# Attention and FP8 feed-forward block: batch 0 ahead of the other batches, maxima half a batch ahead of the exponentials, and shift rows copied in quarters

## The reference

```python
    x = L0_attn_X
    xn = _layernorm(x, axis=-1)
    x = x + _L0_attn_ref(xn, W_q, W_k, W_v, W_o) + _L0_ffn_ref(xn, weight, bias)

    # attention: Qr, Kr are the rotated projections, per head of width 16
        scores = jnp.einsum('bhqd,bhkd->bhqk', Qr, Kr) * DH ** (-0.5)
        scores = jnp.where(causal[None, None], neg, scores)
        pattern = jax.nn.softmax(scores, axis=-1)
        heads = jnp.einsum('bhqk,bhkd->bhqd', pattern, Vh)
        out = heads.transpose(0, 2, 1, 3).reshape(b, t, d)
        return out @ W_o.T
    # linear layer
        def fake_quant_fp8(t):
            amax = jnp.max(jnp.abs(t))
            scale = FP8_E4M3_MAX / jnp.maximum(amax, 1e-12)
            q = (t * scale).astype(jnp.float8_e4m3fn).astype(jnp.float32)
            return q / scale
        xq = fake_quant_fp8(x); wq = fake_quant_fp8(weight)
        return jnp.einsum('bsd,od->bso', xq, wq) + bias
```

## Time and profile before

| | us |
|---|---|
| median of 3 runs | 468.52 (466.98 to 469.78) |
| the profiled execution's own time | 468.62 |
| its span | 466.9 |
| PE busy | 405.5 (87%) |
| DVE busy | 350.1 (75%) |
| ACT busy | 277.3 (59%) |
| POOL busy | 274.4 (59%) |

### The profile page before, as it was taken

One profiled execution on the slowest core, in us unless ns is written; L12 is line 12 of the kernel. 1 busy time (PEld: TensorE's weight loads), 2 busy tenths in 40 slices (PEclk: granted clock), 3 DMA queues, 4 the chain that ended last, 5 costly groups with the idle time before them and its releaser, 6 DMA issues.

```text
span 466.9 us, 9145 instructions
## 1 busy us (share of the span) xinstructions
PE 405.5 (87%) x2819; PEld 222.8 (48%) x2819; DVE 350.1 (75%) x1340; ACT 277.3 (59%) x500; POOL 274.4 (59%) x278
## 2 busy tenths in 40 slices
PE   1790676999889999999999999999999999998975
PEld 1440521364345556654565556555655545643443
DVE  3779899969769977997799778977897878842041
ACT  2742932147765677567666765677567656675850
POOL 2304376636746984698459844985498337226552
PEclk9996555599999999999999999999999999999999
DMA  7826747300483238422851375037504760020021
GB/s 234 257 87 197 159 136 193 81 5 18 143 214 84 69 101 204 131 69 78 216 144 46 93 213 152 32 110 206 158 18 124 194 170 2 4 93 3 1 91 46
DMA packets 37617, 53.43 MB, mean 114 GB/s; under 512 B 5152, under 2 KB 31136, under 8 KB 37536
## 3 DMA queue, kind: packets, MB, share of 16 engines
q1 hardware_dynamic: 37568, 52.84, 40.6%
HBM read 35.78 MB, written 17.04 MB: 113 GB/s over the span
## 4 chain that ended last, share of the span: by engine, by line
PE 44%; POOL 22%; ACT 11%; issue 10%; DVE 8%; DMA 3%; POOLq 1%; SPq 1%; ACTq 0%; DVEq 0%
PE st_ps L842 10%; PE o_ps L922 9%; PE s_ps L860 7%; ACT prob L722 6%; PE m_ps L894 5%; PE m_ps L869 4%; POOL prob L427 4%; POOL rot L259 4%; PE m_ps L798 4%; POOL rot L253 3%; DVE scratch L587 3%; POOL xq L457 3%; POOL parts L263 3%; POOL rot L252 2%; POOL qv L453 2%
## 5 line engine op out<-in xcount | busy, mean ns | idle before, releaser
L587 DVE CUSTOM_DVE_ANT_0 scratch<-s_ps,causal 128x512 bf16<-128x512 f32 (+3 forms) x512 | 220.9, 485 | 55.0 <-PE s_ps L860 52.9
L722 ACT ACTIVATE prob<-st_ps 128x512 f32<-128x512 f32 x320 | 174.8, 600 | 97.9 <-PE st_ps L842 97.4
L427 POOL TENSOR_SCALAR_AFFINE_SELECT prob<-prob 128x512 f32<-128x512 f32 (+1 forms) x160 | 86.4, 544 | 130.9 <-ACT prob L722 129.4
L860 PE MATMUL s_ps<-k_st,q_st 96*128 96x512 bf16 (+3 forms) x512 | 130.8, 320 | 7.0 <-DVE rowmax L587 3.2
L842 PE MATMUL st_ps<-q_st,k_st 98*128 98x128 bf16 (+3 forms) x512 | 121.9, 303 | 4.2 <-ACT prob L722 2.8
L922 PE MATMUL o_ps<-prob,v_sb 128*17 128x512 f32 (+3 forms) x1024 | 87.4, 437 | 10.0 <-ACT heads L737 5.1
L842 PEld LDWEIGHTS st_ps<-q_st,k_st 98*128 98x128 bf16 x512 | 42.0, 97 | 76.3 <-ACT prob L722 42.3
L860 PEld LDWEIGHTS s_ps<-k_st,q_st 96*128 96x128 bf16 x512 | 48.9, 99 | 43.7 <-DVE rowmax L587 20.6
L922 PEld LDWEIGHTS o_ps<-prob,v_sb 128*17 128x17 f32 x1024 | 20.5, 96 | 48.3 <-issue 36.0
L587 DVE DVE_READ_ACCUMULATOR2_ANT rowmax<- 128x1 f32 x512 | 41.7, 81 | 0.1
L894 PE MATMUL m_ps<-wo_sb,attnT 128*128 128x256 f32 x128 | 33.2, 381 | 1.8 <-DVE x_res L610 1.4
(11 more groups left out here) (99 smaller groups left out, 502.6 us busy)
## 6 DMA issues: line engine op xcount, KB each, us to landing
qk_parts<-parts SPq DMA_DIRECT2D x16, 768.0 KB, 3.7
q_st<-qk_parts SPq DMA_DIRECT2D x32, 192.0 KB, 3.3
k_st<-qk_parts SPq DMA_DIRECT2D x32, 192.0 KB, 3.7
q_st<-x_dram SPq DMA_DIRECT2D x8, 512.0 KB, 5.5
q_st<-qk_parts SPq DMA_DIRECT2D x32, 128.0 KB, 3.4
k_st<-qk_parts SPq DMA_DIRECT2D x32, 128.0 KB, 3.7
x_res<-x_dram SPq DMA_DIRECT2D x8, 512.0 KB, 3.5
out_dram<-x_res SPq DMA_DIRECT2D x8, 512.0 KB, 4.8
```

The source lines that it names most:

```text
L427: eng.affine_select(out=ap, in_=ap, compare_op=ALU.is_ge, fill=0.0, base=0, pattern=pat, channel_multiplier=-1).then_inc(masked, 1)
L587: eng.tensor_tensor_reduce(scratch[:, at, col:col + w], s_ps[at][:, col:col + w], causal[:, T - w:T], 1.0, NEG, ALU.add, ALU.max, rowmax[: ...
L722: eng.activation(prob[u][:, half * T:(half + 1) * T], st_ps[ST_BANK[2 * s + half]][:, :], ACT.Exp, scale=SCALE).then_inc(exp_done, 1)
L860: mm = eng.matmul(bank[:, col:col + (qb + 1) * P], q_st[0:ROWS, 1 - par, h, qb * P:(qb + 1) * P], k_st[0:ROWS, 1 - par, h, 0:(qb + 1) * P] ...
```

## The change

Time is counted in slots of the exponentials: slot 20n+s is slot s of batch n. The lists now run from slot -10 to 175.

- **Start.** Only batch 0 is normalised, turned, projected and split first, with its parts handled in halves, on DVE and POOL; batch 1 is normalised beside it. The statistics, normalising and turning of batches 3 to 7 stand in the slots -9 to 8 (`LATE_NORM` is the slot of the turning), that of batch 2 just ahead. The largest value per batch (`largest`) follows in the odd slots 1 to 15, the scales in slots 16 to 20.
- **Maxima** run 10 slots ahead of the exponentials (`LEAD`), where it was 20. Slots -10 to -1 hold maxima alone.
- **The table** `OFFSETS` takes the place of `MISC`: the slot of each item relative to its batch's first. `o`, `at` and `fin` come 2 to 5 slots sooner, `qk` stands in every second slot from 10 to 16, `mt` is in four quarters of 16 columns (two halves of 32 before).
- **Rounding** of batch n moves from slots 20 to 26 of its count to 16 to 20 (`quant_slot`); batch 0's is at 23 to 27.
- **Rotation and split** on POOL move from slots 3 to 13 of an iteration to slots 13 to 22 (`rotate` at 13 and 18, `remainder` 15 and 20, `low` 17 and 22).
- **Shift rows** go from SBUF to SBUF, two DMAs a quarter (write and read through DRAM before, in halves).
- **Stacks** are written as before and read in halves of 8 heads, at slots 0, 3, 5 and 8 of the batch before (groups of 4 heads before): 12 reads a batch where there were 24.
- **End.** The last batch's output is stored in four parts.

```diff
+OFFSETS = {("v", 0): 0, ("mt", 1): 1, ("v", 1): 2, ("o", 0): 23, ("o", 1): 24, ("o", 2): 25, ("mt", 2): 6, ("o", 3): 26,
+           ("at", 0): 26, ("at", 1): 27, ("fin", 0): 28, ("at", 2): 29, ("fin", 1): 30, ("qk", 0): -30, ("mt", 3): 11,
+           ("at", 3): 31, ("fin", 2): 32, ("qk", 1): -28, ("qk", 2): -26, ("fin", 3): 34, ("qk", 3): -24, ("mt", 0): -4}
+LATE_NORM = {2: -8, 3: -6, 4: -4, 5: -2, 6: 3, 7: 7}
...
+def quant_slot(n):
+
+    return 23 if n == 0 else SLOTS * n + 16
...
+            def write_parts(n, w):
+
+                eng.wait_ge(low_done[w], 2 * n + 2)
+                eng.dma_start(qk_dram[n % 2, w].rearrange("t r j h n -> (j h) (t r) n"),
+                              parts[:, w].rearrange("p t r n -> p (t r) n")).then_inc(parts_out[w], 16)
...
+            def shift_rows(n, g):
+
+                c = NG * n + g
+                eng.wait_ge(shift_done, c + 1)
+                for t in range(SHIFT):
+                    eng.dma_start(q_st[ROWS + t:ROWS + t + 1, n % 2, g * HG:(g + 1) * HG, :],
+                                  shift[:, t, :]).then_inc(shift_in[c % 2], 16)
...
+                for off, step, w in ((-27, rotate, 0), (-25, remainder, 0), (-23, low, 0),
+                                     (-22, rotate, 1), (-20, remainder, 1), (-18, low, 1)):
+                    n = batch_at(slot, off, 1)
+                    if n is not None:
+                        step(eng, n, w)
...
+                for n in quant_at(slot, 2):
+                    eng.wait_ge(qc_done, n + 1)
+                    eng.tensor_tensor(qv[:, :], qv[:, :], qe[:, :], ALU.add).then_inc(qw_done, 1)
+                for n in quant_at(slot, 4):
+                    eng.wait_ge(qw_done, n + 1)
+                    wait_past(eng, full["fin"], 4 * n)
+                    eng.tensor_tensor(xq.rearrange("p c t -> p (c t)"), qv[:, :], qe[:, :],
+                                      ALU.subtract).then_inc(xq_done, 1)
```

More of the change, by code:

```diff
@@ L61, in wait_past @@
         eng.wait_ge(sem, count)
-def each_batch(eng, step, between):
-    for n in range(NB):
-        step(n, n % 2)
-        between(n)
 def unit_parts(u, half):
@@ L198, in attention_ffn_block @@
         s_full = sem("s_full")
-        full = {k: sem(f"{k}_full") for k in ("qk", "v", "o", "at", "fin", "mt")}
+        full = {k: sem(f"{k}_full") for k in ("qk", "v", "o", "at", "fin", "mt", "spread", "ln")}
         pv_done = sem("pv_done")
@@ new lines, in _ @@
+            statistics(0)
+            statistics(1)
+            eng.wait_ge(w_qk_in, 16 * 4)
+            rope(0, 0, first_ps[0])
+            rope(0, 1, first_ps[1])
+            rotate(eng, 0, 0)
+            rope(0, 2, first_ps[2])
+            rope(0, 3, first_ps[3])
+            rotate(eng, 0, 1)
+            remainder(eng, 0, 1)
+            low(eng, 0, 1)
+            statistics(2)
+            for slot in range(FIRST_SLOT, END_SLOT):
+                at = maximum_slot(slot)
+                if at is not None:
+                    n, s = at
+                    row_max(n, 2 * s)
+                    row_max(n, 2 * s + 1)
+                for n in range(3, NB):
+                    if slot == LATE_NORM[n] - 3:
+                        statistics(n)
+                if slot in range(1, 2 * NB, 2):
+                    largest(slot // 2)
+                weight_step(slot)
+                for kind, n, k in shared_at(slot, "qk", "o", "fin", "mt"):
+                    {"qk": rope, "o": norm, "fin": finish, "mt": split_max}[kind](n, k, shared[kind, n, k])
+                for n in quant_at(slot, 1):
+                    eng.wait_ge(qv_done, n + 1)
+                    eng.tensor_scalar(qe[:, :].bitcast(U32), qv[:, :].bitcast(U32), 0x7F800000, None,
+                                      ALU.bitwise_and).then_inc(qe_done, 1)
+                    eng.wait_ge(qe_done, n + 1)
+                    eng.tensor_scalar(qe[:, :], qe[:, :], 2.0 ** -6, 1.5 * 2.0 ** 20, ALU.max, ALU.mult)\
+                       .then_inc(qc_done, 1)
@@ new lines, in high_x, with exp @@
+            def high_x(n):
+                wait_past(eng, full["qk"], 4 * n if n > 1 else 0)
+                eng.copy(x_parts[:, 0], xnT[:, n]).then_inc(x_high, 1)
+            def exp(n, s):
+                g, u = divmod(s, 5)
+                if n > 0 or g > 0:
+                    eng.wait_ge(pv_done, 12 * n + 3 * (g - 1) + (1, 1, 2, 2, 3)[u])
+                for half in range(2):
+                    eng.wait_ge(st_full, 2 * (SLOTS * n + s) + half + 1)
+                    eng.activation(prob[u][:, half * T:(half + 1) * T], st_ps[ST_BANK[2 * s + half]][:, :],
+                                   ACT.Exp, scale=SCALE).then_inc(exp_done, 1)
@@ new lines, in copy_at @@
+            def copy_at(n, qb, bank):
+                eng.wait_ge(full["at"], 4 * n + qb + 1)
+                wait_past(eng, full["fin"], 4 * n + max(qb - 1, 0))
+                eng.copy(attnT[:, qb % 2, :, :], bank[:, 0:D].rearrange("p (c n) -> p c n", c=NC))\
+                   .then_inc(at_copied, 1)
+            nw = NC * D
+            normalise(0)
+            copy_turned(0)
+            normalise(1)
+            high(0, 0)
+            copy_turned(1)
+            middle(0, 0)
+            high(0, 1)
@@ L974, in _, with scores @@
-            run(iteration)
+            def scores(n, s, between):
+                g, u = divmod(s, 5)
+                if u == 0:
+                    c = NG * n + g
+                    eng.wait_ge(shift_in[c % 2], 32 * (c // 2 + 1))
+                for half in range(2):
+                    i = 2 * s + half
+                    wait_past(eng, exp_done, HALVES * n + ST_BEFORE[i] + 1)
+                    for j, kb, col in unit_parts(u, half):
+                        h = g * HG + j
+                        mm = eng.matmul(st_ps[ST_BANK[i]][:, col:col + T - kb * P],
+                                        k_st[0:ROWS + SHIFT, n % 2, h, kb * P:(kb + 1) * P],
+                                        q_st[0:ROWS + SHIFT, n % 2, h, kb * P:T], start=True, stop=True)
+                    mm.then_inc(st_full, 1)
+                    if half == 0:
+                        between()
```

996 lines of the change are left out of this document (451 added, 545 removed).

## The result

| | before | after |
|---|---|---|
| median of 4 runs each | 468.04 us (466.98 to 469.78) | 525.78 us (524.48 to 526.42) |
| ratio, 95% interval | | 1.123 (1.118 to 1.127) |
| span of the profiled execution | 466.9 us | 524.2 us |
| mean granted clock | 0.938 | 0.909 |

The kernel is 12.3% slower. The prediction had the sign, slower, but its time was 480, its range ended at 490, and 57.7 us were lost where it said 12.

What follows compares the result with a forecast made beforehand. PE bounds the middle, DVE the start's maxima. 121.5 to slot 20, 236.3 middle, 17.5 and 3.7 added there, 42.7 and 40.0 for batches 6 and 7, 16.5 tail: 478.2, plus 1.7 is 480 us; range 463 to 490.

Steps and rivals of the forecast that it cites:

- The start: Up to slot 20: first maximum at 40.5, slot 0 at 67.0, slot 20 at 121.5 instead of 134.3, a gain of 12.8.
- Slots -10 to -1: Maxima ahead of slot 0: DVE 25.0 us, PE 29.8 at half clock; 26.5 taken, between 25 and 30.
- Batch 0: Slots 0 to 19: DVE's work sums to 53.1 us, 1.4 for waits makes 54.5, where it took 44.5.
- Rival (c): PE's clock stays at half in batch 0: slot 20 at 144, time 503 us; chance 0.03.
- (e): The start isn't won, first maxima wait for the reads until 50: 489 us; chance 0.12 together with Rival (d).
- Direct copies and larger stack reads: Shift rows from SBUF to SBUF and stack reads of 8 heads: 0 each; far end for the copies 1 a batch.
- Rival (d): The direct copies of the shift rows come late: 7 us more, 487 us; chance 0.12 together with (e).
- Part 1: Middle, slots 17 to 23: POOL's 13.9 us chain makes PE wait 3.0 a batch, with 0.6 more through ACT and DVE.
- the mask in slot 23: Sign in the middle: PE waits over 2 us a batch for the mask, at the products with V.
- `qe`: Rounding on DVE in slot 17, beside `low`: contention counted as 0.65, as beside POOL's rotation (1.34 against 0.69 alone).
- Part 2: Slot 6: `at` waits for `split_max`, a bank passed on in the same slot, 1.3 a batch.
- the first `fin`: Once, in slot 28: held by POOL's second addition and the bias sum, 2.7.

Runs made afterwards that it cites:

- e1: The changed kernel with the second halves of Q's and K's stacks read 12 and 6 slots ahead, not 17 and 12: 502.32 us, ratio 1.071.
- e4: The changed kernel with twelve extra PE products before the wait for the third quarter of the shift rows, batches 2 to 6: 516.40 us, ratio 1.099.
- e10: e6 with ScalarE's scaling for the rounding back in slot 16 instead of 17: 478.51 us, ratio 1.020.
- e11: e10 with batches 2 and 3 normalised and turned, batch 3's statistics and three `largest` computed ahead of the first maximum: 472.47 us, ratio 1.006.
- e5: e1 with the rounding of batches 1 to 7 spread over slots 17 to 25, the two `qe` apart: 485.60 us, ratio 1.037.
- e6: e5 with the first transpose of the attention output in slot 27 instead of 26: 479.05 us, ratio 1.021.
- e3: The changed kernel with all steps of the rounding one slot sooner: 523.22 us, ratio 1.114.

## Why the prediction was wrong

**The start: order right, 6.8 us too early.** The first maximum was late by 2.5 us: the first half of K was issued at 34.5 and landed at 43.0, on full engines (share 1.05), with both second halves issued behind it by 38.5. I had 7.3 us for the reading back; it took 8.5 and began 1.3 us later than I had it. Slots -10 to -1 took 30.6, just above the end of my bracket of 25 to 30: PE waited 7.8 us there for rotation products that stand on DVE behind statistics, in a bank that it needed in the same slot. I had summed each engine by itself and taken a value near the larger sum; in a stretch where two engines pass banks back and forth, each has gaps that the other's queue makes. Batch 0 was right to 0.2 us, partly by luck: DVE was busy for 50.1 us, not 53.1, and idle for 4.6, not 1.4. Its busy share was 92%, where the prediction had named over 95% as the sign. Rival (c), half a clock through batch 0, didn't come (0.95), and (e) came in part.

**Direct copies and larger stack reads, both costed at nothing: the step that failed.** "Larger stack reads: 0, they are 3 us or more early" asked whether the stacks are in time, and they were. It didn't ask what else is in the DMA engines while they run. In batch 4 of the new order three half reads of 768 KB each are issued from 313.6 to 322.7, and the split of the third quarter (slot 6) and its use (slot 10) lie in the time that these take. Rival (d) had the right place of trouble but a price from the wrong row: it took 3.7 us, a large transfer alone in the earlier trace rows, as the longest a copy could take, and up to 9.1 us are what a copy took beside the reads. e1 puts the price of this step at 23.5 us. No run reads the stacks in groups of 4 heads again, so what their size did, apart from their place, isn't shown.

**The clock, left out of the middle.** I used the clock for the start and for rival (c), and charged waits in the middle at their length. PE's waits of 2.7 to 3.9 us were followed by stretches at half. In the middle the clock is 0.92 over 288.7 us, so that some 46 us passed at half and some 23 us of work were lost, beside the 33 us of waits themselves. e4 shows this by itself: more work in the wait, less time.

**Part 1, POOL's chain: found, smaller, and hidden behind something else.** It costs 1.44 a batch (e10, e11), through ScalarE, where I had 3.0 at the mask and 0.6 for ScalarE and DVE. In the changed kernel it doesn't show, I suppose because PE waits longer, 2.70, for DVE in the same slots. The prediction named the mask in slot 23 as its sign, and POOL made no PE wait there.

**`qe`: the rule was right and the row that I took was not the case at hand.** I weighed 0.65 us of contention from the earlier trace rows against the whole `low`, and let the sum stay. `qe` began 0.11 us behind `low` and took 2.58: its own 0.68 and the remaining 2.02 of `low` give 2.70. Beside the shorter rotations it took 1.4 to 1.8, alone 0.67. The Trainium skill, "SBUF — State Buffer", section "SBUF: two separate sides", says that of DVE and POOL the one that starts first on their shared port pair keeps it for its whole instruction, and the other waits. The trace agrees: 2.58 us, with 2.70 by that rule. The row of 1.34 was a `qe` that started at 240.81 beside a rotation of 1.27 us begun at 240.33; what was left of that, 0.79, is about the 0.65 that I took for a constant. With the clock and the row of maxima behind it, this step and the place of the rounding cost 16.7 us (e5), where I had 0.6 a batch, some 3 us in all, for it and ScalarE together.

**Part 2, a bank passed on in the same slot: right.** 1.3 a batch was said, 1.14 measured, with DVE's split as releaser, and e6 gets 6.6 us back for it. It is the one new wait that the order alone made plain. Of what comes once, PE's wait in front of the first `fin` was 0.5 and not 2.7.

In numbers, from the changed kernel on: 23.5 us for the stack reads beside the shift rows, 16.7 for the rounding, 6.6 for the bank, 6.0 for work that the start could have done while it waited, and 0.5 from e6 to e10, which is within noise. That leads from 525.8 to 472.5. 3 us over before remain. The middle of e11 loses 2.4 us a batch against before, 12 in all, which takes back the 12 us by which its slot 20 is earlier (V projection at 123.4 against 135.3), and from 371.6 to the end it takes 99.2 us where before took 96.3 from 370.6.

## What to carry over

When a small transfer gets a place in the order, ask what the DMA engines carry between its issue and its use, not only how long such a transfer takes; a second queue doesn't help against a full load. In a stretch that PE bounds, charge a wait of some 3 us with the clock behind it as well, unless a row shows that the clock stays: 3.1 us more in the changed kernel behind one of 3.04 us, 1.7 in e3 behind waits of 3.0 to 3.7 (a clock of 0.72 over 6.2 us of work). Work moved next to another engine's long instruction takes its price from that instruction, so use the row with the same partner and the same order of starting, and look for idle time at the start that can take work over: that was worth 6.0 us here (e11).
